# Barriers between the stages of a transformer block on eight cores, replaced by waits on single semaphores

## The chip, the cores and the metric

The kernel runs on all 8 cores of one Trainium2 chip. Each core computes two of the 16 sequences and shares nothing with the others. The metric is the device time of the slowest core, in microseconds (us), as the median over runs.

## The reference

One layer in the macaron form, on x of 16 x 2048 x 1024:

```python
x = x + 0.5 * ffn(layernorm(x))
x = x + attn(layernorm(x))
x = x + 0.5 * ffn(layernorm(x))
```

`ffn` is itself an attention, with 16 heads of width 64. A router (softmax of the mean of x @ Wr) picks 4 heads per sequence and a gate for each; Q, K and V of these four, times the gate, go through full softmax attention, and the 256 columns through Wo. `attn` is differential attention:

```python
q = apply_rotary(rmsnorm(x @ Wq.T), cos, sin) / sqrt(64)   # 16 half heads
k = apply_rotary(rmsnorm(x @ Wk.T), cos, sin)
attn = softmax(causal(q @ k))                              # 2048 x 2048
attn = attn[:, :, 0] - lam * attn[:, :, 1]                 # 8 heads
out = layernorm(attn @ v) * (1 - LAMBDA_INIT)
return out @ Wproj.T
```

## The kernel before, in words

`emit_all` (L1083) writes the program of each engine as a list; `wait` (L173) puts a wait for a semaphore's value into an engine's list. Each engine goes through its list in order. There is a semaphore for each of TensorE (`self.PE`), ScalarE (`self.ACT`), VectorE (`self.DVE`) and GpSimd (`self.GPS`), counted up by their instructions. A DMA is issued from a queue: SyncE (`sp`, 8 channels in turn), GpSimd (`gps`, 4) or ScalarE (`act`, 4), and each channel is a semaphore. `wait_q` (L205) makes an engine wait for all DMAs so far of one queue. `barrier` makes every engine wait for all 20 semaphores at the values that they have at this place in the program, 20 waits in each list (fewer where a semaphore is still at 0).

```python
    def barrier_into(self, eng):
        for s in self.ALLSEM:
            self.wait(eng, s, s.n)
```

`ALLSEM` lists TensorE, ScalarE, VectorE, GpSimd, the channels of SyncE, those of GpSimd and those of ScalarE, in this order. DMAs that change the type (weights from float32 in HBM to bfloat16) are issued from GpSimd, DMA transposes from SyncE or ScalarE. `dma` issues at L195, `dmat`, the transpose, at L202; so every DMA has one of these two lines.

For each of the two sequences (batches) of a core:

1. x is loaded into `x_res` and stays there; a layer norm writes bfloat16 tiles to `lnx_d`, and eight transposes (`_ln_transposes`) bring them back as `reg_a`.
2. First FFN, written out in `emit_all`: router, the folding of the chosen heads' weights into `wselg` (`emit_wfold`), projections (`emit_ffn_qkv`: L523 for Q and K, L549 for V), attention in two pairs of heads and eight blocks of queries (`emit_ffn_attn`: scores L580, exponentials on ScalarE L592, times V L612), and the output (`emit_ffn_out`: store of `zstrip`, two transposes, L670), with the next layer norm's sums beside it and the transposes behind it. attn_wqT and attn_wkT are loaded there into `big_b`.
3. `emit_attn`: the transposes a second time, Q and K projections for 16 tiles of tokens (L759) with norm and rotation on VectorE and GpSimd, then attn_wvT into `big_b` and the V projection (L782). `emit_attn_core` goes through eight heads: transposes of Q and K into `qk_strm`, scores (L926) against the blocks allowed by the mask, exponentials (L946), times V (L967), fix-ups on VectorE, sixteen strips of normalisation per head (L1022), and a store to `zhat_d`. `emit_attn_out`: eight transposes of `zhat_d` into `big_b` from SyncE, attn_wpT into `wselg` and ffn_wqT into `qk_strm` from GpSimd, and the output projection (L1052), again with the sums of the next norm beside it.
4. `emit_ffn` for the second FFN, as the first, but with the transposes a second time, too; then y is stored.

Between these parts stand barriers. `emit_all` has them ahead of each part of the first FFN and behind it; `emit_attn` and `emit_ffn` have one at their start, ahead of each part and at the end. Two stand in a row where `emit_all`'s or `emit_attn`'s last meets the first of the next.

Of the kernel before, what the change touches and what calls it, by code (L numbers as in the profile page):

```python
# [76 lines left out]
class MK:  # L77
# [286 lines left out]
    def _ln_transposes(self):  # L364
        P = self
        P.wait_q("act", "act")
        P.wait_q("act", "sp")
        for c in range(NC):
            P.dmat("act", self.reg_a[:, c * S:(c + 1) * S], self.lnx_d[:, c * 128:(c + 1) * 128])
# [143 lines left out]
    def emit_ffn_qkv(self, b, ci):  # L513
        P = self
        evac_ms = [0, 0]
        for wi, dst, bslot in ((0, self.qsel, 0), (1, self.ksel, 2)):
# [128 lines left out]
    def emit_ffn_out(self, b, ci, fuse_ln=None):  # L645
        P = self
# [4 lines left out]
        zt = self.qk_strm[:, 0:2 * S]  # L651
        for c in range(2):
            P.dmat("sp", zt[:, c * S:(c + 1) * S], self.zffn_d[:, c * 128:(c + 1) * 128])
        P.dma("gps", self.qk_strm[:, 4096:6144].rearrange("p (c f) -> p c f", f=D), self.w["ffn_wo"].rearrange("(c p) f -> p c f", p=128))
        P.dma("gps", self.rowsb[0:1, 0:1024], self.w["ffn_bo"][None, :])
        wo = self.qk_strm[:, 4096:6144]
        if getattr(self, "_prefetch_attn_w", False):
            P.dma("gps", self.big_b[:, 0:NC * D].rearrange("p (c f) -> p c f", f=D),
                  self.w["attn_wqT"].rearrange("(c p) f -> p c f", p=128))
            P.dma("gps", self.big_b[:, NC * D:2 * NC * D].rearrange("p (c f) -> p c f", f=D),  # L660
                  self.w["attn_wkT"].rearrange("(c p) f -> p c f", p=128))
        P.wait_q("pe", "sp")
        P.wait_q("pe", "gps")
        res_ms = [0, 0]
# [26 lines left out]
    def emit_ffn(self, b, ci, skip_ln=False, next_ln=None, wq_prefetched=False):  # L691
        P = self
        self.barrier()
# [29 lines left out]
        self.barrier()  # L723
        self.emit_ffn_qkv(b, ci)
        self.barrier()
        self.emit_ffn_attn(b, ci)
        self.barrier()
# [3 lines left out]
    def emit_attn_qkv(self, b, w_prefetched=False):  # L731
        P = self
# [7 lines left out]
        P.wait_q("pe", "gps")  # L740
        wbq = self.big_b[:, 0:NC * D]
# [290 lines left out]
    def emit_attn_out(self, b, fuse_ln=None):  # L1032
        P = self
# [6 lines left out]
        if getattr(self, "_prefetch_ffn_w", False):  # L1040
            P.dma("gps", self.qk_strm[:, 0:8192].rearrange("p (c f) -> p c f", f=D),
                  self.w["ffn_wqT"].rearrange("(c p) f -> p c f", p=128))
# [26 lines left out]
    def emit_attn(self, b, skip_ln=False, next_ln=None, w_prefetched=False):  # L1069
        self.barrier()  # L1070
        if skip_ln:
            self._ln_transposes()
        else:
            self.emit_ln(b, with_router=False, tag=f"attn_{b}")
        self.barrier()
        self.emit_attn_qkv(b, w_prefetched=w_prefetched)
        self.barrier()
        self.emit_attn_core(b)
        self.barrier()
# [134 lines left out]
```

How the kernel before makes its waits and increments, by code:

```python
    def wait(self, eng, sem, val):  # L173
        if val > 0:
            self.q[eng].append(lambda e, s=sem, v=val: e.wait_ge(s.h, v))
# [15 lines left out]
    def dma(self, queue, out, in_, **kw):  # L191
        ch = self._chan(queue)
        v0 = ch.n
        self.on(queue, lambda e, o=out, i=in_, s=ch, w=v0, kw=kw: (
            e.wait_ge(s.h, w), e.dma_start(out=o, in_=i, **kw).then_inc(s.h, 16)))
        return ch, ch.inc(16)
# [1 line left out]
    def dmat(self, queue, out, in_):  # L198
        ch = self._chan(queue)
        v0 = ch.n
        self.on(queue, lambda e, o=out, i=in_, s=ch, w=v0: (
            e.wait_ge(s.h, w), e.dma_start_transpose(o, i).then_inc(s.h, 16)))
        return ch, ch.inc(16)
# [8 lines left out]
        def step(e, f=fn, s=sem, w=w):  # L212
            e.wait_ge(s.h, w)
            f(e).then_inc(s.h, 1)
# [12 lines left out]
    def pe(self, fn, inc=True):  # L227
        if inc:
            self.on("pe", lambda e, f=fn, s=self.PE: f(e).then_inc(s.h, 1))
            return self.PE.inc(1)
        self.on("pe", fn)
        return self.PE.n
```

## Time and profile before

| | us |
|---|---|
| median of the 2 timed runs | 4664.37 (4661.91 and 4666.83) |
| the profiled execution, its own time | 4639.7 |
| its span, core 6, the slowest | 4638.1 |
| spans of the eight cores | 4594.9 to 4638.1 |
| busy in the span: TensorE | 2575.3 |
| VectorE | 1446.3 |
| ScalarE | 1467.0 |
| GpSimd | 332.1 |

The profile is of one execution on its slowest core. "Busy" leaves out waits and DMA issues. The chain of waits is followed back from the last instruction, at each step to what released it; a piece "ACTq" or "SPq" is a queue's own instruction, L175 a wait, L202 a transpose's issue, "issue" is time in which nothing that the profile shows was waited for. PEclk, or granted clock, is TensorE's as a share of 2.4 GHz; DMA share is the busy share of the core's 16 DMA engines. Times count from the start of the span.

### The profile page before, as it was taken

The page shows a single profiled execution, that of the slowest core. Times are in us where ns is not written, and L with a number is a line of the kernel's source. Part 1 is how long each engine was busy: PE and PEld are TensorE (multiplying, and loading weights), DVE is VectorE, ACT ScalarE, POOL GpSimd, SP SyncE. Part 2 cuts the span into 40 slices and gives each one's busy share as a digit, 9 for nine tenths or more (in the row PEclk, how much of TensorE's full clock was granted, in tenths as well). Part 3 has the DMA queues.
Part 4 walks back from the last instruction along what each step waited for, and adds up shares of the span by engine and source line. Part 5 has one row for each costly group of instructions (what it writes and reads, how often), then busy time and mean ns, then how long its engine had stood idle before and what let it go on. Part 6 is the DMA issues. An engine that isn't in the chain of part 4 may idle for free.

```text
span 4638.1 us, 58267 instructions; the slowest of 8 cores (4594.9 to 4638.1 us)
## 1 busy us (share of the span) xinstructions
PE 2575.3 (56%) x18326; PEld 1257.5 (27%) x18326; DVE 1446.3 (31%) x3373; ACT 1467.0 (32%) x1602; POOL 332.1 (7%) x258
## 2 busy tenths in 40 slices
PE   2367426556565645277523775264565666443875
PEld 0134202124343311244101341021233434102441
DVE  3121135623333333121231212366234333331212
ACT  1007313305555510027110173133055545100370
POOL 0000005610000000000000000066000000000000
PEclk9575558777767777575565755587777767776655
DMA  4310340031101042500243103400301020424003
GB/s 115 71 19 2 60 109 30 37 87 21 37 19 37 6 77 60 85 1 1 89 124 64 19 1 60 109 35 36 86 19 37 19 37 6 77 70 76 1 1 96
DMA packets 421276, 224.72 MB, mean 48 GB/s; under 512 B 358230, under 2 KB 366678, under 8 KB 420978
## 3 DMA queue, kind: packets, MB, share of 16 engines
q1 hardware_dynamic: 214610, 109.55, 9.3%
q10 hardware_dynamic: 180224, 67.13, 6.4%
q0 software_dynamic: 26144, 44.31, 6.2%
q8 instruction: 158, 2.59, 0.2%
q14 instruction: 140, 1.15, 0.1%
HBM read 114.20 MB, written 79.76 MB: 42 GB/s over the span
## 4 chain that ended last, share of the span: by engine, by line
PE 36%; DVE 19%; ACT 15%; DMA 10%; issue 9%; ACTq 6%; SPq 3%; DVEq 1%; POOL 0%; POOLq 0%
ACT big_b L946 6%; ACT big_b L592 6%; PE pw L967 5%; ACTq L202 5%; PE pw L612 3%; PE pw L926 3%; SPq L202 3%; PE pw L670 3%; PE pw L523 3%; PE pw L1052 2%; PE pw L782 2%; PE pw L478 2%; PE pw L580 2%; PE pw L352 2%; PE pw L350 2%
## 5 line engine op out<-in xcount | busy, mean ns | idle before, releaser
L946 ACT ACTIVATE big_b<-pw,c 128x1024 bf16<-128x1024 f32 x576 | 641.2, 1113 | 667.3 <-PE pw L926 224.7
L592 ACT ACTIVATE big_b<-pw 128x1024 bf16<-128x1024 f32 x512 | 523.8, 1023 | 745.2 <-PE pw L580 719.2
L967 PE MATMUL pw<-vstrips,big_b 128*128 128x129 bf16 x4352 | 433.4, 256 | 432.8 <-ACT big_b L946 180.9
L967 PEld LDWEIGHTS pw<-vstrips,big_b 128*128 128x128 bf16 x4352 | 329.5, 115 | 564.9 <-issue 564.7
L759 PE MATMUL pw<-big_b,reg_a 128*128 128x512 bf16 x1024 | 280.8, 442 | 308.5 <-DMA reg_a<-lnx_d 167.2
L612 PE MATMUL pw<-vstrips,big_b 128*128 128x65 bf16 x4096 | 307.7, 241 | 156.0 <-ACT big_b L592 96.6
L926 PE MATMUL pw<-qk_strm 64*128 64x256 bf16 x2304 | 320.7, 330 | 33.8 <-DMA vstrips<-vhat_d 33.7
L612 PEld LDWEIGHTS pw<-vstrips,big_b 128*128 128x128 bf16 x4096 | 237.9, 126 | 359.5 <-issue 359.5
L580 PE MATMUL pw<-qk_strm 64*128 64x256 bf16 x2048 | 298.3, 404 | 10.6 <-issue 10.6
L317 ACT ACTIVATE scr<-x_res 128x1024 f32<-128x1024 f32 x96 | 101.4, 1057 | 545.1 <-DVE stats L315 418.8
L350 PE MATMUL pw<-scr,c 128*1 128x512 f32 x128 | 88.2, 779 | 281.6 <-DVE qk_bf L348 217.4
L759 PEld LDWEIGHTS pw<-big_b,reg_a 128*128 128x128 bf16 x1024 | 110.2, 110 | 479.1 <-issue 398.7
L635 DVE RECIPROCAL stats<-pw 128x2 f32<-128x2 f32 x128 | 21.9, 171 | 619.3 <-PE pw L612 612.6
L994 DVE RECIPROCAL stats<-pw 128x2 f32<-128x2 f32 x128 | 21.8, 171 | 609.1 <-PE pw L967 542.0
L670 PE MATMUL pw<-qk_strm 128*128 128x512 bf16 x256 | 132.1, 620 | 134.2 <-issue 116.7
L1052 PE MATMUL pw<-wselg,big_b 128*128 128x512 bf16 x512 | 115.0, 389 | 133.2 <-issue 66.9
L782 PE MATMUL pw<-big_b,reg_a 128*128 128x512 bf16 x512 | 114.9, 389 | 116.9 <-DMA big_b<-attn_wvT 116.9
L382 ACT COPY scr<-pw 1x512 f32<-1x512 f32 x4 | 2.3, 574 | 502.2 <-DMA reg_a<-lnx_d 502.2
L683 DVE SCALAR_TENSOR_TENSOR x_res<-pw,x_res 128x512 f32<-128x512 f32 x128 | 88.5, 692 | 195.9 <-PE pw L675 188.5
L315 DVE TENSOR_REDUCE stats<-x_res 128x1 f32<-128x1024 f32 x96 | 117.1, 1220 | 98.7 <-DMA x_res<-x 89.0
L478 PE MATMUL pw<-wselg,big_b 128*128 128x256 bf16 x640 | 96.6, 326 | 72.1 <-DMA big_b<-ffn_wkT 35.2
L926 PEld LDWEIGHTS pw<-qk_strm 64*128 64x128 bf16 x2304 | 101.7, 104 | 127.7 <-issue 81.1
(172 smaller groups left out, 2761.8 us busy)
## 6 DMA issues: line engine op xcount, KB each, us to landing
x_res<-x SPq DMA_DIRECT2D x2, 8192.0 KB
y<-x_res SPq DMA_DIRECT2D x2, 8192.0 KB
lnx_d<-qk_bf ACTq DMA_DIRECT2D x48, 256.0 KB, 2.0
lnx_d<-pt ACTq DMA_DIRECT2D x48, 256.0 KB, 2.1
vstrips<-vhat_d SPq DMA_DIRECT2D x16, 516.0 KB
big_b<-ffn_wkT POOLq DMA_DIRECT2D x4, 2048.0 KB, 17.4
big_b<-ffn_wvT POOLq DMA_DIRECT2D x4, 2048.0 KB, 23.1
zhat_d<-zstrip SPq DMA_DIRECT2D x16, 512.0 KB
```

The lines of the kernel that those rows point to most:

```text
L202: e.wait_ge(s.h, w), e.dma_start_transpose(o, i).then_inc(s.h, 16)))
L478: P.pe(lambda e, fs=fs, mc=mc, bank=bank: e.matmul(bank[:, 0:256], wb[:, mc * D + fs * 128: mc * D + (fs + 1) * 128], self.gsel[:, mc * 25 ...
L580: P.pe(lambda e, hp=hp, qh=qh, kt=kt, ki=ki, hi=hi, pw=pw: e.matmul(pw[:, hi * 512 + ki * 256:hi * 512 + (ki + 1) * 256], self.ksel[hi * 6 ...
L592: P.act(lambda e, pw=pw, g=g: e.activation(out=self.big_b[:, (g % 4) * 1024:(g % 4) * 1024 + 1024], in_=pw[:, 0:1024], func=AF.Exp, scale= ...
L612: first=first, last=last: e.matmul(ob[:, qi * 65:(qi + 1) * 65], self.big_b[:, (g % 4) * 1024 + hi * 512 + ki * 256 + qi * 128: (g % 4) * ...
L670: P.pe(lambda e, tt=tt, half=half, c=c, bank=bank: e.matmul(bank[:, 0:512], zt[:, c * S + tt * 128:c * S + (tt + 1) * 128], wo[:, c * 1024 ...
L759: P.pe(lambda e, tt=tt, fc=fc, half=half, bank=bank, wb=wb: e.matmul(bank[:, 0:512], self.reg_a[:, fc * S + tt * 128:fc * S + (tt + 1) * 128],
L782: P.pe(lambda e, tt=tt, fc=fc, half=half, bank=bank, wb=wb: e.matmul(bank[:, 0:512], self.reg_a[:, fc * S + tt * 128:fc * S + (tt + 1) * 128],
L926: qT=qT, kT=kT, is_last=is_last: e.matmul(pw[:, hi * 512 + ki * 256:hi * 512 + (ki + 1) * 256], kT[hi * 64:(hi + 1) * 64, kt * 128:(kt + 1 ...
L946: P.act(lambda e, pw=pw, g=g: e.activation(out=self.big_b[:, (g % 4) * 1024:(g % 4) * 1024 + 1024], in_=pw[:, 0:1024], func=AF.Exp, scale= ...
L967: vst=vst, first=first, last=last: e.matmul(ob[:, qi * 129:(qi + 1) * 129], self.big_b[:, (g % 4) * 1024 + hi * 512 + ki * 256 + qi * 128: ...
L1052: P.pe(lambda e, tt=tt, fc=fc, half=half, bank=bank: e.matmul(bank[:, 0:512], self.big_b[:, fc * S + tt * 128:fc * S + (tt + 1) * 128], wp ...
```

## The change

Eight barriers per batch go: the first of `emit_attn` and of `emit_ffn` (kept where the layer norm isn't skipped, which doesn't occur here), and in both those ahead of each part behind it. Waits of single engines take their place, in the callers and inside `_ln_transposes`, `emit_ffn_qkv`, `emit_ffn_out`, `emit_attn_qkv` and `emit_attn_out`. The barriers of `emit_all`, around the first FFN, and those at the end of `emit_attn` and `emit_ffn` stay. The diff in full:

```diff
@@ -365,6 +365,7 @@
         P = self
         P.wait_q("act", "act")
         P.wait_q("act", "sp")
+        P.wait("act", self.PE, self.PE.n)
         for c in range(NC):
             P.dmat("act", self.reg_a[:, c * S:(c + 1) * S], self.lnx_d[:, c * 128:(c + 1) * 128])
 
@@ -513,6 +514,7 @@
     def emit_ffn_qkv(self, b, ci):
         P = self
         evac_ms = [0, 0]
+        P.wait("pe", self.DVE, self.DVE.n)
         for wi, dst, bslot in ((0, self.qsel, 0), (1, self.ksel, 2)):
             base = wi * NC * 256
             for h in range(2):
@@ -649,18 +651,22 @@
               self.zstrip.rearrange("p (t c) -> p t c", c=256))
         P.wait_q("sp", "sp")
         zt = self.qk_strm[:, 0:2 * S]
+        P.wait("sp", self.PE, self.PE.n)
         for c in range(2):
             P.dmat("sp", zt[:, c * S:(c + 1) * S], self.zffn_d[:, c * 128:(c + 1) * 128])
+        P.wait("gps", self.PE, self.PE.n)
         P.dma("gps", self.qk_strm[:, 4096:6144].rearrange("p (c f) -> p c f", f=D), self.w["ffn_wo"].rearrange("(c p) f -> p c f", p=128))
         P.dma("gps", self.rowsb[0:1, 0:1024], self.w["ffn_bo"][None, :])
         wo = self.qk_strm[:, 4096:6144]
         if getattr(self, "_prefetch_attn_w", False):
+            P.wait("gps", self.PE, self.PE.n)
             P.dma("gps", self.big_b[:, 0:NC * D].rearrange("p (c f) -> p c f", f=D),
                   self.w["attn_wqT"].rearrange("(c p) f -> p c f", p=128))
             P.dma("gps", self.big_b[:, NC * D:2 * NC * D].rearrange("p (c f) -> p c f", f=D),
                   self.w["attn_wkT"].rearrange("(c p) f -> p c f", p=128))
         P.wait_q("pe", "sp")
         P.wait_q("pe", "gps")
+        P.wait("pe", self.DVE, self.DVE.n)
         res_ms = [0, 0]
         for tt in range(NT):
             P.wait("pe", self.DVE, res_ms[tt % 2])
@@ -690,7 +696,8 @@
 
     def emit_ffn(self, b, ci, skip_ln=False, next_ln=None, wq_prefetched=False):
         P = self
-        self.barrier()
+        if not skip_ln:
+            self.barrier()
         if skip_ln:
             self._ln_transposes()
         else:
@@ -720,11 +727,13 @@
             P.wait_q("pe", "gps")
             self.emit_wfold(2, "ffn_bv", 4, slot=0)
         self.tap(f"wsel_{b}_{ci}", self.wsel[:, :])
-        self.barrier()
+        P.wait("pe", self.DVE, self.DVE.n)
+        P.wait_q("pe", "act")
         self.emit_ffn_qkv(b, ci)
-        self.barrier()
+        P.wait("pe", self.DVE, self.DVE.n)
+        P.wait("act", self.DVE, self.DVE.n)
         self.emit_ffn_attn(b, ci)
-        self.barrier()
+        P.wait("pe", self.DVE, self.DVE.n)
         self.emit_ffn_out(b, ci, fuse_ln=next_ln)
         self.barrier()
 
@@ -738,6 +747,7 @@
             P.dma("gps", self.big_b[:, NC * D:2 * NC * D].rearrange("p (c f) -> p c f", f=D),
                   self.w["attn_wkT"].rearrange("(c p) f -> p c f", p=128))
         P.wait_q("pe", "gps")
+        P.wait("pe", self.DVE, self.DVE.n)
         wbq = self.big_b[:, 0:NC * D]
         wbk = self.big_b[:, NC * D:2 * NC * D]
         ev_q = [0, 0]
@@ -1038,6 +1048,7 @@
                    self.zhat_d.rearrange("(h t p) d -> h (t p) d", h=NH, p=128)[c])
         P.dma("gps", self.wselg[:, 0:8192].rearrange("p (c f) -> p c f", f=D), self.w["attn_wpT"].rearrange("(c p) f -> p c f", p=128))
         if getattr(self, "_prefetch_ffn_w", False):
+            P.wait("gps", self.PE, self.PE.n)
             P.dma("gps", self.qk_strm[:, 0:8192].rearrange("p (c f) -> p c f", f=D),
                   self.w["ffn_wqT"].rearrange("(c p) f -> p c f", p=128))
         P.wait_q("pe", "sp")
@@ -1067,16 +1078,21 @@
             self._ln_finish(with_router=(fuse_ln == "router"))
 
     def emit_attn(self, b, skip_ln=False, next_ln=None, w_prefetched=False):
-        self.barrier()
         if skip_ln:
             self._ln_transposes()
         else:
+            self.barrier()
             self.emit_ln(b, with_router=False, tag=f"attn_{b}")
-        self.barrier()
+        P = self
+        P.wait("pe", self.DVE, self.DVE.n)
+        P.wait_q("pe", "act")
         self.emit_attn_qkv(b, w_prefetched=w_prefetched)
-        self.barrier()
+        P.wait_q("sp", "sp")
+        P.wait("dve", self.GPS, self.GPS.n)
         self.emit_attn_core(b)
-        self.barrier()
+        P.wait_q("sp", "sp")
+        P.wait("sp", self.PE, self.PE.n)
+        P.wait("act", self.PE, self.PE.n)
         self.emit_attn_out(b, fuse_ln=next_ln)
         self.barrier()
```

No instruction changes its place on its engine; what changes is what it waits for. Where the waits stand out, the instruction lists show them in brackets, `s_` for an engine's semaphore and `d_` for a channel's.

SyncE, end of the attention core in the first batch (`zhat_d<-zstrip` are the stores of heads, `big_b<-zhat_d` the transposes for the output projection), with - and + for before and now:

```order
 L195 DMA zhat_d<-zstrip 128x16x128 [waits s_dve,d_sp2]
 L195 DMA zhat_d<-zstrip 128x16x128 [waits s_dve,d_sp3]
-L202 DMA_TRANSPOSE big_b<-zhat_d 128x2048 [waits s_pe,s_act,s_dve,s_gps,d_sp0,d_sp1,d_sp2,d_sp3,d_sp4,d_sp5,d_sp6,d_sp7,d_gp0,d_gp1,d_gp2,d_gp3,d_ac0,d_ac1,d_ac2,d_ac3]
+L202 DMA_TRANSPOSE big_b<-zhat_d 128x2048 [waits d_sp0,d_sp1,d_sp2,d_sp3,d_sp4,d_sp5,d_sp6,d_sp7,s_pe]
 L202 DMA_TRANSPOSE big_b<-zhat_d 128x2048 [waits d_sp5]
 L202 DMA_TRANSPOSE big_b<-zhat_d 128x2048 [waits d_sp6]
```

The first transpose still waits for the last store's channel, and for TensorE, but for no load of GpSimd or ScalarE.

GpSimd, from the last rotation of K to the loads of the second FFN, first batch, before:

```order
L865 TENSOR_TENSOR vstrips<-vstrips,sinb_bf 128x512 [waits s_gps]
L866 TENSOR_TENSOR vprod<-vstrips 128x16x32 [waits s_gps]
L195 DMA big_b<-attn_wvT 128x8x1024 [waits s_pe,d_gp1]
L195 DMA wselg<-attn_wpT 128x8x1024 [waits s_pe,s_act,s_dve,s_gps,d_sp0,d_sp1,d_sp2,d_sp3,d_sp4,d_sp5,d_sp6,d_sp7,d_gp0,d_gp1,d_gp2,d_gp3,d_ac0,d_ac1,d_ac2,d_ac3]
L195 DMA qk_strm<-ffn_wqT 128x8x1024 [waits d_gp3]
```

and now:

```order
L875 TENSOR_TENSOR vstrips<-vstrips,sinb_bf 128x512 [waits s_gps]
L876 TENSOR_TENSOR vprod<-vstrips 128x16x32 [waits s_gps]
L195 DMA big_b<-attn_wvT 128x8x1024 [waits s_pe,d_gp1]
L195 DMA wselg<-attn_wpT 128x8x1024 [waits d_gp2]
L195 DMA qk_strm<-ffn_wqT 128x8x1024 [waits s_pe,d_gp3]
```

attn_wpT has lost the waits that stood between it and attn_wvT, among them those for the core's end; ffn_wqT waits for TensorE's last matmul of the core.

TensorE, start of FFN attention in the second FFN, first batch (L549 and L554, now L551 and L556, are the last tile of V, L580, now L582, the first scores), before:

```order
L549 MATMUL pw<-wselg,reg_a 128x256 [waits s_dve]
L549 MATMUL pw<-wselg,reg_a 128x256 x7
L554 MATMUL pw<-rowsb,cbf 128x256
L580 MATMUL pw<-qk_strm 128x256 [waits s_pe,s_act,s_dve,s_gps,d_sp0,d_sp1,d_sp2,d_sp3,d_sp4,d_sp5,d_sp6,d_sp7,d_gp0,d_gp1,d_gp2,d_gp3,d_ac0,d_ac1,d_ac2,d_ac3]
L580 MATMUL pw<-qk_strm 128x256 x7
```

and now:

```order
L551 MATMUL pw<-wselg,reg_a 128x256 [waits s_dve]
L551 MATMUL pw<-wselg,reg_a 128x256 x7
L556 MATMUL pw<-rowsb,cbf 128x256
L582 MATMUL pw<-qk_strm 128x256 [waits s_dve]
L582 MATMUL pw<-qk_strm 128x256 x7
```

Of twenty waits one is left, for VectorE.

## Rows read from the trace of the kernel before

**Rows 1.** The page, part 4: shares of the chain of waits by engine

```profile
PE 36%; DVE 19%; ACT 15%; DMA 10%; issue 9%; ACTq 6%; SPq 3%; DVEq 1%; POOL 0%; POOLq 0%
```

**Rows 2.** Chain of waits, end of the first attention core: start us, us, what

```profile
1644.37 4.86 DMA zhat_d<-zstrip
...
1650.35 2.12 SPq L202
...
1652.57 14.03 SPq L202
...
1666.69 14.01 SPq L202
...
1692.99 4.68 DMA big_b<-zhat_d
...
1698.65 57.61 PE pw L1052 x256
```

**Rows 3.** Timeline of GpSimd: start us, us, engine, line, operation, idle before

```profile
1650.56 0.87 POOL L195 DMA_DIRECT2D wselg<-attn_wpT  x1 [699.60 <-issue]
```

**Rows 4.** DMA issues in 1640 to 1702 us: size, us from issue to landing

```profile
wselg<-attn_wpT POOLq DMA_DIRECT2D x1, 2048.0 KB, 16.9
qk_strm<-ffn_wqT POOLq DMA_DIRECT2D x1, 2048.0 KB, 29.2
```

**Rows 5.** Busy time by stretch (engines, granted clock, DMA share, GB/s)

```profile
core 6: us, PE busy (x) PEld busy (x) DVE busy (x) ACT busy (x) POOL busy (x), PEclk, DMA share, GB/s
...
1650.35:1697.67 47.32, 0.00 (x0) 0.00 (x0) 0.00 (x0) 0.00 (x0) 1.75 (x2) 0.50 1.07 177
1840.86:1864.17 23.31, 0.00 (x0) 0.00 (x0) 0.00 (x0) 0.00 (x0) 0.00 (x0) 0.55 0.95 180
1866.34:1913.71 47.37, 0.00 (x0) 0.00 (x0) 0.00 (x0) 0.00 (x0) 1.38 (x2) 0.50 1.03 170
```

**Rows 6.** Timeline of TensorE and VectorE at the end of the core

```profile
1631.88 0.51 PE L967 MATMUL pw<-vstrips,big_b 128*128 128x129 bf16 x6 [1.01 <-ACT big_b L946]
...
1637.56 6.67 DVE L1022 TENSOR_SCALAR zstrip<-zstrip,stats 128x128 bf16<-128x128 bf16 x16 [1.03 <-ACT stats L1017]
```

**Rows 7.** Chain of waits, the same place in the second batch

```profile
3958.28 3.82 DMA zhat_d<-zstrip
3963.32 3.24 SPq L202
...
4007.65 4.35 DMA big_b<-zhat_d
```

**Rows 8.** Chain of waits, load of attn_wvT ahead of the V projection

```profile
950.02 14.17 DMA big_b<-attn_wvT
964.64 57.68 PE pw L782 x256
```

**Rows 9.** Chain of waits, ScalarE queue, two barriers in a row, first and last

```profile
1864.19 0.02 ACTq L175
...
1866.29 0.02 ACTq L202
```

**Rows 10.** Chain of waits, TensorE behind the barriers of the second FFN

```profile
1978.17 0.14 issue
...
1979.19 2.33 issue
...
2040.27 2.10 issue
```

**Rows 11.** Chain of waits on SyncE behind FFN attention, first and last

```profile
2224.88 0.02 issue
...
2225.84 0.02 SPq L195
```

**Rows 12.** Busy time by stretch around the start of FFN attention

```profile
2042.00:2046.00 4.00, 2.35 (x32) 1.40 (x32) 0.00 (x0) 2.85 (x3) 0.00 (x0) 0.80 0.00 0
2042.40:2225.00 182.60, 142.16 (x1536) 79.04 (x1536) 23.63 (x96) 130.96 (x128) 0.00 (x0) 0.51 0.01 1
```

## The prediction

> **What bounds the kernel now.** I began with the spans of the cores (4594.9 to 4638.1 us, so all eight behave alike), then the page's chain of waits, then that chain in order of time. No engine bounds the whole: TensorE has 36% of the chain, VectorE 19%, ScalarE 15% [rows 1]; the work goes through stages with a barrier between them. So I looked for stretches in which no engine works. In the chain in order of time the longest is at the end of the attention core. The last matmul of the core ends at 1632.39 us and VectorE's last strip at 1644.23 [rows 6]. Then come the store of the last head (4.86 us), eight DMA transposes issued from 1650.35, of which two each hold the queue 14 us, and the first matmul of the output projection at 1698.65 [rows 2]. GpSimd had been idle for 700 us and issued attn_wpT and ffn_wqT at 1650.56 and right behind it [rows 3]; they landed 16.9 and 29.2 us later [rows 4]. The DMA engines are full in that stretch (share 1.07). Eight transposes of the same size with nothing beside them took 23.3 us, and eight beside two such weight loads 47.4 us [rows 5]. The second batch has the same picture [rows 7].
>
> **The change, part by part.** All durations are from one profiled execution of 4639.7 us (span 4638.1), 24.7 us under the median of the runs shown, 4664.4; a saving worked out in the first is taken off the second.
>
> *The end of the core.* The barrier ahead of emit_attn_out goes. On GpSimd's queue attn_wpT now stands directly behind attn_wvT, with no wait but its own channel's: it is issued near 951 us instead of 1650, and a load alone lands in 14.2 us [rows 8], so it lies beside the V projection (57.7 us [rows 8]), which needs the queues little. ffn_wqT overwrites qk_strm, which the core reads, so it waits for TensorE alone and not for VectorE and the store: issued near 1632.6 instead of 1651.4. Alone it would land between 1632.6 + 14.2 = 1646.8 (the row of attn_wvT) and 1632.6 + 16.9 = 1649.5 (attn_wpT's, which had company). Both are before 1650.35. So the eight transposes lose both companions: 47.32 us become 23.3, a gain of 24.0. Against it, ffn_wqT now shares the DMA engines with the last store for 2.4 to 5.1 us; the store can be late by none of it or all; I take 2 us. The wait list of the first transpose becomes shorter (21 waits after the store in 1.1 us before, 14 after): 0.4 us. The first batch gains 24.0 - 2 + 0.4 = 22.4 us. In the second the stretch was 3963.32 to 4012.00, 48.7 us [rows 7], so 48.7 - 23.3 - 2 + 0.4 = 23.8. Together 46.2 us. Bounds: 50.6 with no delay of the store and 0.4 more per batch, and below, if only one of the two loads leaves the stretch, half of 24.0 + 25.4, which is 24.7.
>
> *Loads moved, and what they pass.* What attn_wpT could hurt is attn_wvT just ahead of it, for which TensorE waits. Two loads issued together landed 12.3 us apart [rows 4], so they go one after the other; I take 0. The bounds are 0 and 12.0 us per batch. Ahead of ffn_wo only TensorE is waited for now, some 4 us earlier; it lies beside a store and two transposes: 0.
>
> *The waits themselves.* A barrier is up to 20 waits on each engine. Where all were long satisfied they still cost issue time: on ScalarE 34 waits of two barriers and what follows took 2.1 us [rows 9], some 0.055 us each; on SyncE, behind FFN attention, 18 in 0.96 us [rows 11]. The doubled barriers ahead of emit_attn's and emit_ffn's transposes stand on the chain on ScalarE: 20 waits less and one more each, 2 x 1.05 = 2.1 us per batch. TensorE is slower at it: it took 2.33 us from VectorE's last write to the first matmul of the FFN's projections and 2.10 us to that of FFN attention, where a single wait costs 0.14 us [rows 10]. 17 waits followed the one on VectorE, so about 0.12 each; six remain in the first place (0.8 us with the 0.14) and one in the second (0.2): 1.5 + 1.9 = 3.4 us. SyncE ahead of the FFN's store 0.9 us; ahead of the core 0.3. The barrier ahead of attn_qkv costs nothing, since ScalarE's channels, the last of its list, are what TensorE waits for there either way. Sum 6.7 us per batch, 13.4 for two. Bounds: 4 (TensorE's waits overlapping other latency) and 16.
>
> *Waits added.* TensorE on VectorE, ScalarE on TensorE and on VectorE, SyncE on TensorE, VectorE on GpSimd: each stands where the store, the transposes or the load ahead lands later than what it asks for, or where a barrier stays. Behind ScalarE's wait ahead of the transposes stand only these; it asks for matmuls that end before the last store has landed. I take 0 and bound it at 0.5 us each, the core's last group of matmuls [rows 6].
>
> Sum: 46.2 + 13.4 = 59.6 us, so 4639.7 becomes 4580.1, and 4664.4 becomes 4604.8.
>
> The Trainium skill, "SBUF — State Buffer", section "SBUF: two separate sides", says that a DMA issued from GpSimd has its descriptors written by GpSimd, and that VectorE in a two-port mode locks it out of the ports for it, so that the DMA sits and waits. VectorE runs sixteen bf16 strips from 1637.56 to 1644.23 in this stretch, 5 us after the new issue of ffn_wqT [rows 6]. By that rule the load could stand still until 1644.2 and run beside the transposes; no run here has such a load beside such strips. By the sum without it the load has landed by then.
>
> **The rivals.**
> 1. Only attn_wpT leaves the stretch; ffn_wqT starts, but moves its bytes only once VectorE's strips are done at 1644.2, and still lies beside the transposes. For it: VectorE is busy through most of the new window [rows 6]. Against: they begin 5 us after the issue, and GpSimd's part of an issue took 0.87 us [rows 3]. Gain at the core 24.7: 24.7 + 13.4 = 38.1, time 4626. The rule quoted above would give this. The same price, within 3 us, if attn_wvT is slowed by the load behind it (59.6 - 24.0 = 35.6, time 4629). Together 0.18.
> 2. The change doesn't do what it says: the transposes of zhat_d are slow by themselves, and not for the loads. Against: the two of 14 us stand exactly beside the loads, and once the second of them is through, at 1680.7, all that is left lands within 17 us [rows 2]. Then only 13.4 + 0.8 are gained, time 4650. Chance 0.05.
> 3. Slower than before, through TensorE's clock: the output projection took 57.6 us for 256 matmuls [rows 2], 225 ns each, after a start at the low level. If it ran whole at half the granted clock, with 450 ns each, it would take 57.6 us more per batch, 115 in all: 4604.8 + 115 = 4720, slower than before. It decides once more than half of the two projections (59.6 of 115 us) runs so. Against: TensorE idles there before and after the change, and the shorter idle time gives no reason to stay low. Chance 0.02.
> 4. Faster, through the clock at the start of FFN attention: the granted clock was 1.00, 0.80 on average in the first 4 us, and 0.51 over the stage's 182.6 us [rows 12]. Just ahead TensorE stood idle, 2.1 us of it behind the barrier [rows 10], of which the change leaves 0.2. If the clock stays at 2.4 GHz, the stage is bound by ScalarE's 131 us [rows 12] and by the 16 drains between blocks of queries, say 1 us each, so 147: 35 us in each of the two second FFNs, 70 in all, time 4535. But the slowest of eight cores would have to keep it for both stages, and each drain can end it. Chance 0.04. A part of it on some cores doesn't show in the slowest.
>
> **How the numbers follow.** My forecast has 0.71. The low end takes 50.6 + 16 = 67 us off, 7 more than the forecast, and then 30 for what one execution differs from another (4639.7 to 4666.8 in the three shown) and for a core that keeps the clock for part of FFN attention: 4568. The high end is the first rival with some 14 us for the spread: 4640. It leaves out rivals 2 to 4, 0.11. About 2%, 93 us, is what a measurement of this kernel tells from no change. Only rival 4 passes it below: 0.04. Nothing named passes 4758 above; 0.01 for what I don't see. The rest, 0.95, lies within.
>
> **What would show it.** In the changed kernel: attn_wpT issued right behind attn_wvT near 950 us and landed before 980; ffn_wqT issued within 1 us of the core's last matmul; the eight transposes of zhat_d in 23 to 25 us, none with 14; the first matmul of the output projection some 43 us after the core's last instead of 66; TensorE's gap ahead of FFN attention, in the second FFN alone, near 1 us. Wrong: a load that lands after the first transposes have begun, a store of zhat_d over 8 us, an attn_wvT of over 20 us, or FFN attention in the second FFN at another clock than in the first.

## The result and the profile after

| | before | changed |
|---|---|---|
| median, us | 4643.3 (10 runs) | 4562.18 (11 runs, 4556.66 to 4604.97) |
| ratio, 95% interval | 1 | 0.9843 [0.9808, 0.9877] |
| the changed kernel run again with the experiments, us | 4646.96 (11 runs) | 4559.92 (6 runs, ratio 0.9832 [0.9782, 0.9883]) |
| busy in the span: TensorE, VectorE, ScalarE, GpSimd | 2575.3, 1446.3, 1467.0, 332.1 | 2559.8, 1447.3, 1468.1, 331.9 |

0.9843 of 4643.3 is a saving of 73 us, 57 to 89 by its interval; forecast were 59.6. It lies within 2%, as forecast; the second series gives 78 us, with an interval that reaches a little beyond 2%. In some executions of either kernel the cores of one die show a lower granted clock and the time is longer, which the ratios leave out, and as the first profiled execution of the changed kernel was one of them, the rows below are from the second series (4558.45 us; core 0, the slowest).

The page, its header, part 1 and part 4:

```profile
span 4556.8 us, 56773 instructions; the slowest of 8 cores (4532.1 to 4556.8 us)
...
PE 2559.8 (56%) x18326; PEld 1244.0 (27%) x18326; DVE 1447.3 (32%) x3373; ACT 1468.1 (32%) x1602; POOL 331.9 (7%) x258
...
PE 37%; DVE 19%; ACT 16%; DMA 10%; issue 9%; ACTq 6%; SPq 2%; DVEq 1%; POOL 0%; POOLq 0%
```

Busy times are as they were but for 16 us of TensorE. The transposes' issues ("SPq") have gone from 3% of the chain to 2% [rows 1]: the work is the same, and a piece of the waiting is gone.

The chain of waits at the end of the attention core (start us, us, what), first batch, and in the second:

```profile
1642.23 4.98 DMA zhat_d<-zstrip
...
1647.98 2.05 SPq L202
...
1650.12 2.71 SPq L202
...
1663.48 2.14 SPq L202
...
1665.71 4.09 DMA big_b<-zhat_d
...
1670.81 56.99 PE pw L1063 x256
...
3905.28 7.11 DMA zhat_d<-zstrip
...
3915.16 3.48 SPq L202
...
3932.75 4.24 DMA big_b<-zhat_d
```

These answer to [rows 2] and [rows 7]. Where two transposes held the queue 14 us each, all eight of the first batch now hold it 2.0 to 2.7 us, and from the first issue to the last landing pass 1669.80 - 1647.98 = 21.8 us instead of 47.3. It is the same on the eight cores in both batches: before, the second and the third transpose held the queue 12.4 to 18.5 us each (once 25.2); now none holds it more than 3.9, and the eight take 20.2 to 25.4 us. The first matmul of the projection comes 1670.81 - 1630.27 = 40.5 us behind the core's last:

```profile
1629.76 0.51 PE L977 MATMUL pw<-vstrips,big_b 128*128 128x129 bf16 x6 [1.01 <-ACT big_b L956]
1670.81 9.49 PE L1063 MATMUL pw<-wselg,big_b 128*128 128x512 bf16 x36 [40.54 <-issue]
...
1635.45 6.64 DVE L1032 TENSOR_SCALAR zstrip<-zstrip,stats 128x128 bf16<-128x128 bf16 x16 [1.03 <-ACT stats L1027]
```

The columns are start, duration, engine, line, operation, and in brackets the idle time ahead of it, here 40.54 us. VectorE's sixteen strips and what stands before them are as in [rows 6].

DMA issues (size each, us from issue to landing) in 1625 to 1700 us and in 940 to 975 us:

```profile
qk_strm<-ffn_wqT POOLq DMA_DIRECT2D x1, 2048.0 KB, 14.5
...
big_b<-attn_wvT POOLq DMA_DIRECT2D x1, 2048.0 KB, 17.5
wselg<-attn_wpT POOLq DMA_DIRECT2D x1, 2048.0 KB, 27.5
```

And GpSimd's timeline:

```profile
940.60 0.94 POOL L195 DMA_DIRECT2D big_b<-attn_wvT  x1
941.53 0.88 POOL L195 DMA_DIRECT2D wselg<-attn_wpT  x1
...
1630.87 0.88 POOL L195 DMA_DIRECT2D qk_strm<-ffn_wqT  x1 [688.46 <-PE pw L977]
```

attn_wpT stands right behind attn_wvT; ffn_wqT is released by "PE pw L977", the core's last matmul [rows 3, 4]. Both loads are out of the transposes' way, as the prediction has it.

The second FFN. The chain at the start of its projections (first two rows) and of its attention (the other two):

```profile
1947.02 0.17 DVE rowbuf L511
1947.19 0.77 issue
...
2005.53 0.44 DVE vstrips L559
2005.96 0.14 issue
```

From VectorE's last write to the first matmul 0.77 and 0.14 us, instead of 2.33 and 2.10 [rows 10]. And the clock in that attention (busy time by stretch: us, then TensorE, its weight loads, VectorE, ScalarE and GpSimd, each with its count, granted clock, DMA share, GB/s):

```profile
2006.00:2061.00 55.00, 42.97 (x471) 23.87 (x472) 5.91 (x24) 40.29 (x40) 0.00 (x0) 0.52 0.01 1
```

It is at the 1.2 GHz level, as in [rows 12], though the wait ahead of it is gone.

One collision of the same kind is left. At the start of `emit_ffn` the second set of transposes of `lnx_d` runs beside the loads of ffn_wkT and ffn_wvT, as it did before [rows 5, last line]. GpSimd's timeline, then the chain of waits:

```profile
1836.57 0.88 POOL L195 DMA_DIRECT2D big_b<-ffn_wkT  x1 [204.82 <-DMA reg_a<-lnx_d]
...
1836.82 1.27 ACTq L202
1838.17 30.62 ACTq L202
```

The loads wait for the first set of transposes, at the barrier that stays at the end of `emit_attn`, and so start together with the second set.

To see where all of it went I added up, on each of the eight cores, the time between the last matmul of a stage and the first of the next. Medians of the eight, us, first batch / second batch:

| between | before | changed |
|---|---|---|
| core and output projection | 66.8 / 66.2 | 41.1 / 42.0 |
| folding and projections, second FFN | 2.7 / 2.7 | 1.1 / 1.2 |
| projections and attention, second FFN | 2.7 / 2.7 | 0.8 / 0.8 |
| attention and output, second FFN | 20.2 / 19.4 | 18.8 / 18.3 |
| FFN output and Q/K projections of `emit_attn` | 84.3 / 84.1 | 82.9 / 82.6 |
| last norm sum and folding, second FFN | 94.4 / 94.5 | 93.8 / 95.2 |
| Q/K and V projections | 59.6 / 58.7 | 60.8 / 59.7 |
| V projection and core | 16.7 / 16.0 | 16.9 / 15.4 |
| the same two gaps of the first FFN (projections; attention), untouched, first batch | 2.6 and 2.6 | 2.6 and 2.6 |

Without the last row the table is a saving of 60.4 us, 49.9 of it at the end of the core. (In the second batch the first FFN's gap ahead of its projections went from 2.6 to 2.9.) Against the 73 of the ratio, some 13 us have no place in it. They lie within the ratio's interval, and the runs of before that the ratio uses lie up to 61 us apart (4617.0 to 4678.3 in one series).

Part of them is how far the slowest core stands from the others. Between the two profiled executions the slowest span fell by 81.3 us, the median of the eight by 70.1 (4620.1 to 4550.0): the slowest stood 18.0 us above the median before and 6.8 after. Of the 70.1, 60.4 are in the table and about 10 are spread over the rest, 5 of them inside the stages. It is alike in the runs that the second ratio compares: their means differ by 77.9 us, and with the median of the eight cores in place of the slowest by 70.7. "By the median core" means this second reckoning below. Why the slowest core is nearer to the others stays open.

### The profile page after: what moved, and what is told of

It reads as the page before. It is cut to its first block, busy times and chain, and to the rows that moved or that the text cites. A ratio compares the mean times of both kernels' runs of the same rounds, so it can differ in the third digit from the quotient of the medians.

```text
span 4641.7 us, 56709 instructions; the slowest of 8 cores (4560.2 to 4641.7 us)
## 1 busy us (share of the span) xinstructions
PE 2670.6 (58%) x18262; PEld 1286.2 (28%) x18326; DVE 1447.1 (31%) x3373; ACT 1468.2 (32%) x1602; POOL 331.7 (7%) x258
## 4 chain that ended last, share of the span: by engine, by line
PE 39%; DVE 18%; ACT 15%; DMA 10%; issue 9%; ACTq 6%; SPq 2%; DVEq 1%; POOL 0%; POOLq 0%
ACT big_b L956 6%; ACT big_b L594 6%; PE pw L977 6%; ACTq L202 5%; PE pw L936 4%; PE pw L614 3%; PE pw L792 3%; PE pw L1063 3%; PE pw L525 3%; PE pw L676 3%; PE pw L582 2%; PE pw L479 2%; PE pw L352 2%; PE pw L350 2%; DVE zstrip L1032 2%
## 5 line engine op out<-in xcount | busy, mean ns | idle before, releaser
L977 PE MATMUL pw<-vstrips,big_b 128*128 128x129 bf16 x4352 | 456.7, 265 | 417.3 <-ACT big_b L956 181.6
L977 PEld LDWEIGHTS pw<-vstrips,big_b 128*128 128x128 bf16 x4352 | 346.7, 119 | 558.7 <-issue 558.5
L769 PE MATMUL pw<-big_b,reg_a 128*128 128x512 bf16 x1002 | 278.7, 442 | 307.6 <-DMA reg_a<-lnx_d 164.9
L614 PE MATMUL pw<-vstrips,big_b 128*128 128x65 bf16 x4096 | 307.2, 240 | 155.9 <-ACT big_b L594 95.2
L936 PE MATMUL pw<-qk_strm 64*128 64x256 bf16 x2304 | 336.1, 345 | 32.8 <-DMA vstrips<-vhat_d 32.5
L614 PEld LDWEIGHTS pw<-vstrips,big_b 128*128 128x128 bf16 x4096 | 237.0, 125 | 359.5 <-issue 359.5
L582 PE MATMUL pw<-qk_strm 64*128 64x256 bf16 x2048 | 298.3, 404 | 6.7 <-issue 5.2
L1004 DVE RECIPROCAL stats<-pw 128x2 f32<-128x2 f32 x128 | 21.8, 171 | 633.9 <-PE pw L977 555.5
L637 DVE RECIPROCAL stats<-pw 128x2 f32<-128x2 f32 x128 | 21.8, 171 | 614.7 <-PE pw L614 607.9
L792 PE MATMUL pw<-big_b,reg_a 128*128 128x512 bf16 x502 | 137.1, 444 | 123.1 <-DMA big_b<-attn_wvT 122.2
L1063 PE MATMUL pw<-wselg,big_b 128*128 128x512 bf16 x500 | 135.9, 442 | 80.7 <-issue 79.8
```

The costliest lines, as they stand in the source:

```text
L582: P.pe(lambda e, hp=hp, qh=qh, kt=kt, ki=ki, hi=hi, pw=pw: e.matmul(pw[:, hi * 512 + ki * 256:hi * 512 + (ki + 1) * 256], self.ksel[hi * 6 ...
L614: first=first, last=last: e.matmul(ob[:, qi * 65:(qi + 1) * 65], self.big_b[:, (g % 4) * 1024 + hi * 512 + ki * 256 + qi * 128: (g % 4) * ...
L769: P.pe(lambda e, tt=tt, fc=fc, half=half, bank=bank, wb=wb: e.matmul(bank[:, 0:512], self.reg_a[:, fc * S + tt * 128:fc * S + (tt + 1) * 128],
L792: P.pe(lambda e, tt=tt, fc=fc, half=half, bank=bank, wb=wb: e.matmul(bank[:, 0:512], self.reg_a[:, fc * S + tt * 128:fc * S + (tt + 1) * 128],
L936: qT=qT, kT=kT, is_last=is_last: e.matmul(pw[:, hi * 512 + ki * 256:hi * 512 + (ki + 1) * 256], kT[hi * 64:(hi + 1) * 64, kt * 128:(kt + 1 ...
L977: vst=vst, first=first, last=last: e.matmul(ob[:, qi * 129:(qi + 1) * 129], self.big_b[:, (g % 4) * 1024 + hi * 512 + ki * 256 + qi * 128: ...
```

## The experiments

**The changed kernel again.** No edit.

> The changed kernel once more, beside the others. Theory (the loads leave the transposes' stretch: 46 us; queues' waits: 13 us): 60 us under before, ratio 0.987; in its profile the eight transposes of zhat_d take 23 us, ffn_wqT lands before the first of them is issued. Rival (the clock gives part of the gain at the start of FFN attention): 75 us or more under before, and the granted clock of the second FFN's attention is over 0.55 on most cores.

Measured: 0.9832 [0.9782, 0.9883], and the rows above. The 78 us are more than the 75 of the rival, but not by its way: the granted clock over the second FFN's attention is 0.51 on all eight cores.

**Only the end of the core.** In before, the barrier ahead of `emit_attn_out` alone is replaced, with the wait for ffn_wqT:

```diff
         self.emit_attn_core(b)
-        self.barrier()
+        P = self
+        P.wait_q("sp", "sp")
+        P.wait("sp", self.PE, self.PE.n)
+        P.wait("act", self.PE, self.PE.n)
```

> Only the barrier between attention core and output projection is replaced; all others stay. Theory: 46 us of the gain, ratio 0.990, first matmul of the output projection some 43 us behind the core's last. Rival (all removed barriers matter alike, some 8 us each in sum of the engines' restarts): 15 us, ratio 0.997. Rival (the gain needs attn_wpT to be issued as early as behind attn_wvT; here the barrier ahead of the core holds it until near 1027 us): no difference is expected from that by the theory, since it lands 600 us ahead of its use.

Measured: 0.9946 [0.9891, 1.0002], 25 us where 46 were expected, by the time alone not told from none; the gaps between the stages tell more. The stretch at the end of the core did shrink as in the changed kernel, to 41.6 and 41.2 us. But the one ahead of the core, from the V projection to its first matmul, grew from 16.7 to 28.9 and from 16.0 to 27.2 us. GpSimd's timeline and then the chain of waits there (core 2) show why:

```profile
1033.31 0.87 POOL L195 DMA_DIRECT2D wselg<-attn_wpT  x1 [80.99 <-issue]
```

```profile
1032.41 3.39 SPq L202
...
1035.90 12.86 SPq L202
...
1049.48 8.36 DMA qk_strm<-qhat_d
```

The barrier ahead of the core still stands in GpSimd's list between attn_wvT and attn_wpT, so attn_wpT goes out at 1033.31, together with the core's first transposes, and the second of those holds the queue 12.86 us. On all cores and in both batches it is 9.8 to 14.5 us, where the same transpose takes 1.8 to 3.5 in before and in the changed kernel. I had expected nothing from that barrier. In before it costs next to nothing; it costs 12 us per batch once the later one is gone.

**All but the end of the core.** The barrier ahead of `emit_attn_out` is put back into the changed kernel:

```diff
         self.emit_attn_core(b)
+        self.barrier()
         P.wait_q("sp", "sp")
```

> The changed kernel with the one barrier at the core's end put back, ahead of all that follows. Theory: only the queues' waits are saved, 13 us, ratio 0.997, and the stretch from the core's last matmul to the projection is 66 us as before, with two transposes of 14 us. Rival (the rest of the change is worth more than its waits, as the measured 73 us against the forecast 60 may hint): 25 us or more, ratio 0.9945 or less.

Measured: 0.9956 [0.9906, 1.0007], 20 us; the end of the core at 66.4 and 66.3 us, as before, the other gaps of the table 19 us less in sum. 14 of them are in the rows that the forecast names (projections, attention and output of the second FFN, Q/K projections of `emit_attn`), near its 13.4; the other 5 are in rows that move by 1 to 2 us from run to run with no edit there. The two halves add up to 25 + 20 = 45 us by their ratios, the whole is 73 to 78; the 2 x 12 us of the collision ahead of the core, which only the whole avoids, are most of what is missing, though each ratio is known to some 25 us only. By the median core the halves are 27 and 20 us and the whole 71, so 24 are missing.

**The end and the start of the core.** To show that it is this pair, before with these two barriers replaced and no other (and the wait for ffn_wqT, as above):

```diff
         self.emit_attn_qkv(b, w_prefetched=w_prefetched)
-        self.barrier()
+        P = self
+        P.wait_q("sp", "sp")
+        P.wait("dve", self.GPS, self.GPS.n)
         self.emit_attn_core(b)
-        self.barrier()
+        P.wait_q("sp", "sp")
+        P.wait("sp", self.PE, self.PE.n)
+        P.wait("act", self.PE, self.PE.n)
```

> The kernel before with the barriers at both ends of the attention core replaced, all others kept. The run with the core's end alone started the core 12 us later, since attn_wpT was issued with the first transposes of the core. Theory: attn_wpT goes behind attn_wvT again, the wait ahead of the core is 16 us, the one behind it 42, and the gain is 50 us, ratio 0.989. Rival (something else in that run delayed the core): the wait ahead of the core stays at 28 us, ratio 0.9945.

Measured: 0.9893 [0.9845, 0.994], 50 us. The gap ahead of the core is 16.5 and 15.4 us again, its end 42.7 and 40.5, and attn_wpT goes out at once behind attn_wvT, as GpSimd's timeline (core 1) shows:

```profile
952.56 0.94 POOL L195 DMA_DIRECT2D big_b<-attn_wvT  x1
953.50 0.89 POOL L195 DMA_DIRECT2D wselg<-attn_wpT  x1
```

**ffn_wqT late.** In the changed kernel ffn_wqT alone waits for what the barrier asked for, all 20 semaphores as they stand at the end of the core:

```diff
+        at_end = [(s, s.n) for s in self.ALLSEM]
...
         if getattr(self, "_prefetch_ffn_w", False):
-            P.wait("gps", self.PE, self.PE.n)
+            for s, v in at_end:
+                P.wait("gps", s, v)
```

> The changed kernel, but ffn_wqT is issued only when everything up to the core's end is done, the last store included; attn_wpT stays early. Theory (each load beside the transposes costs its own 12 us of full DMA engines): 12 us more per batch than the changed kernel, 24 in all, so 35 us under before, ratio 0.9925; the eight transposes take 35 us, one of them 14. Rival (the transposes suffer only when two loads stand beside them): like the changed kernel, 60 us under before. Rival (one load is as bad as two): 13 us under before.

Measured: 0.9878 [0.982, 0.9936], 57 us; the end of the core 51.1 and 51.8 us, 10 us more than in the changed kernel in each batch. The chain of waits there (core 5), then GpSimd's timeline:

```profile
1653.44 3.87 DMA zhat_d<-zstrip
...
1658.08 2.30 SPq L202
...
1660.48 11.34 SPq L202
```

```profile
1658.63 0.88 POOL L195 DMA_DIRECT2D qk_strm<-ffn_wqT  x1 [706.17 <-issue]
```

One load beside the eight transposes, issued 0.6 us behind the first of them, makes one of them 11.3 us long; two made two of 14 [rows 2]. On the eight cores in both batches it is the second transpose each time, 11.0 to 12.5 us, with 4.0 to 4.4 for the one behind it. So a load beside the transposes costs some 10 us per batch, where 12 were expected; the first rival would have cost that.

**More barriers.** The price of a barrier by itself: before, with three more barriers at each of the seven other places in `emit_attn` and `emit_ffn`.

```diff
+    def more(self):
+        for _ in range(3):
+            self.barrier()
...
         self.barrier()
+        self.more()
         self.emit_ffn_attn(b, ci)
```

> The kernel before, with three more barriers right behind each of its seven that the change drops elsewhere than at the core's end. Theory (a barrier whose semaphores are all reached costs its waits' issue: 1.1 us in a row on ScalarE or SyncE, 2.0 to 2.4 on TensorE): per batch three times 1.1 + 1.1 on ScalarE's places, 2.3 + 2.3 + 2.3 on TensorE's, 1.0 + 1.0 on SyncE's, 33 us, 66 in all, ratio 1.014. Rival (they overlap other latency and are nearly free): under 15 us, ratio under 1.003. Rival (a barrier is a real drain and costs more than its waits): over 120 us.

Measured: 1.0115 [1.0061, 1.0169], 53 us. The gaps at the seven places are 54.6 us longer in sum, where 66 were expected. Per batch: 6.5 ahead of the FFN's projections, 6.4 ahead of its attention, 8.6 and 7.9 ahead of `emit_attn`'s Q/K projections (two places in a row), 2.1 and 2.8 ahead of the core, 2.5 and 1.6 at the start of `emit_ffn`, 1.6 ahead of the FFN's output. In the chain of waits the two on TensorE are:

```profile
2013.35 0.17 DVE rowbuf L514
2013.52 8.82 issue
...
2080.60 0.44 DVE vstrips L561
2081.04 8.47 issue
```

8.82 - 2.33 and 8.47 - 2.10 are 6.5 and 6.4 us for 60 waits: 0.107 us for a wait that is satisfied, 2.1 us for a barrier, on TensorE. Where the chain goes through the lists of SyncE or ScalarE it is a quarter to a half of it: 1.6 / 3 = 0.5 us ahead of the FFN's output, 0.7 to 0.9 ahead of the core. The 8.6 and 7.9 us are of six barriers, three on ScalarE's list ahead of the transposes and three on TensorE's behind them (there 6.71 us pass on core 5 from the last transpose's landing to the first matmul, 0.59 in before).

**One set of transposes.** What the removed barriers left standing in a row: the eight transposes of `lnx_d` are issued twice, with the same result, at the end of the stage and at the start of the next. In the changed kernel the second set goes, in `emit_attn` and likewise in `emit_ffn`:

```diff
-        if skip_ln:
-            self._ln_transposes()
-        else:
+        if not skip_ln:
```

> The changed kernel without the second set of the eight transposes of lnx_d at the start of emit_attn and of emit_ffn (the first set, at the end of the layer norm, has brought the same data). Theory: 24 us less per batch ahead of the attention's projections, and ahead of the second FFN the router starts 47 us earlier, so that its weight loads, 29 us, become what the folding waits for: about 39 us less. Together 63 per batch, 125 in all, so 190 us under before, ratio 0.959. Rival (the loads of ffn_wkT and ffn_wvT stay what counts there): 24 + 10 per batch, ratio 0.972.

Measured: 0.9571 [0.952, 0.9622], near 121 us less than the changed kernel by the medians, 135 by the median core; 125 were expected. The gap ahead of the Q/K projections fell from 82.9 to 58.4 us (57.8 in the second batch), the one at the start of `emit_ffn` from 93.8 and 95.2 to 52.7 and 51.9. That is 24.6 us per batch at the first place and 41 to 43 at the second, 134 in all. At the second more goes than a set costs, since there the set stood beside two loads, as shown above. So a barrier and the second set together were the waste at these two places; the change took the 1 us and left the 24 and more.

**FFN attention with wide V matmuls.** The fourth rival says that this stage would be 35 us shorter at the high clock. In the changed kernel, in all four FFNs, its matmuls with V compute 128 columns instead of 65, of which 63 are not used, so that TensorE has more to do; the block of two outputs lies 256 apart.

```diff
+                                wide = min(128, 4160 - (h * 1040 + kt * 65))
...
-                                    ob[:, qi * 65:(qi + 1) * 65],
+                                    ob[:, qi * 256:qi * 256 + wide],
...
-                                    self.vstrips[:, h * 1040 + kt * 65: h * 1040 + (kt + 1) * 65],
+                                    self.vstrips[:, h * 1040 + kt * 65: h * 1040 + kt * 65 + wide],
```

> The changed kernel with the matmuls with V in both FFN attentions 128 columns wide instead of 65 (the columns beyond are written beside the results and not used), to ask whether TensorE's clock has something to give there. Theory (the clock falls at the stage's start and stays low whatever the matmuls' width): each of the four stages 181 us becomes some 215, the whole 130 us slower than the changed kernel, ratio 1.013. Rival (with wider matmuls TensorE keeps the granted clock at 1.00 for most of the stage): the stage is bound by ScalarE, some 150 us, the whole 120 us faster than the changed kernel, ratio 0.958.

Measured: 0.9775 [0.9724, 0.9826]; neither. Busy time by stretch (core 3), in the first FFN and in the second:

```profile
345.00:400.00 55.00, 38.02 (x496) 24.30 (x496) 8.41 (x35) 42.00 (x42) 0.00 (x0) 1.00 0.01 1
...
2060.00:2110.00 50.00, 34.94 (x460) 22.23 (x454) 7.38 (x30) 39.30 (x39) 0.00 (x0) 1.00 0.01 1
```

The granted clock stays at 2.4 GHz in these stretches; over the four whole stages it is 0.96 to 0.99 on every core, where it was 0.50 to 0.52. TensorE's busy share is 0.69 in the first stretch (0.71 over the whole stages), less than the 0.78 at 1.2 GHz in the rows of the changed kernel; the matmuls compute nearly twice the columns and it is done sooner. But the stage only fell from 181.4 to 170.0 us, not to 147. ScalarE's timeline of one block of queries, up to the first exponentials of the next:

```profile
367.46 2.14 ACT L594 ACTIVATE big_b<-pw 128x1024 bf16<-128x1024 f32 x2 [1.29 <-PE pw L582]
369.89 2.14 ACT L594 ACTIVATE big_b<-pw 128x1024 bf16<-128x1024 f32 x2 [0.28 <-PE pw L582]
372.20 2.14 ACT L594 ACTIVATE big_b<-pw 128x1024 bf16<-128x1024 f32 x2 [0.18 <-ACT big_b L594]
374.52 2.14 ACT L594 ACTIVATE big_b<-pw 128x1024 bf16<-128x1024 f32 x2 [0.17 <-ACT big_b L594]
377.95 2.14 ACT L594 ACTIVATE big_b<-pw 128x1024 bf16<-128x1024 f32 x2 [1.29 <-PE pw L582]
```

A block takes 377.95 - 367.46 = 10.49 us, 16 of them 168: that is the stage. 8.2 us of it are eight exponentials; 1.29 us ScalarE waits for TensorE at the turn of the block, which is the drain (1 was taken), and 1.0 us lies between the exponentials within it, which the estimate of 147 had left out. So a stage at the high clock is shorter, as the fourth rival has it, but with these wider matmuls by 11 us and not by 35: 43 in the four stages. What it would gain with matmuls of 65 columns at the high clock no run shows, nor whether the width holds the clock or the new place of the outputs. By the ratios the run is worth 26 us against the changed kernel, 31 by the medians, with intervals of some 24 us on each, and 42 by the median core.

**Both, and the first FFN too.** The wide V matmuls with one set of transposes, then also the three barriers inside the first FFN, in `emit_all`, replaced by the waits that the second has:

```diff
...
             if phases >= 5:
-                self.barrier()
+                self.wait("pe", self.DVE, self.DVE.n)
+                self.wait("act", self.DVE, self.DVE.n)
                 self.emit_ffn_attn(b, 0)
...
```

> The changed kernel with one set of transposes only and with matmuls with V 128 columns wide: what the runs so far point to. Theory (stages stand one behind the other, so the gains add): ratio 0.957 from the one set, and 11 us less in each of four FFN attentions, 44 in all, so ratio 0.948, 240 us under before. Rival (the wide matmuls' gain was partly chance, as its ratio to the changed kernel, 0.994, is only 28 us): ratio 0.951.

> The same, and the three barriers of the first FFN are replaced as in the second. Theory (its waits alone are saved): 1.5 + 2.0 + 1.3 = 4.8 us per batch, 10 in all, below what a measurement tells, but seen in the profile: 1.1 us instead of 2.6 ahead of the first FFN's projections and 0.75 instead of 2.6 ahead of its attention, on all cores. Rival (the load of attn_wqT and attn_wkT, issued earlier now, delays the store of zffn_d): the wait behind the first FFN's attention, 45 us, becomes longer and eats the 10 us.

Measured: 0.9441 [0.9404, 0.9478], 4378.2 us, and 0.9431 [0.9394, 0.9469], 4373.85 us. The first is the sum of its parts within the intervals (0.9571 less what the wide matmuls gave, 26 to 43 us, is 0.951 to 0.948, and the parts' own intervals are 0.005 to either side). The second step is 4 us by the medians, not told apart from none; in its trace the gaps of the first FFN are 1.1 and 0.75 us instead of 2.6 and 2.6, which makes some 7 us for two batches. The gap behind the first FFN's attention, which the rival has longer, is 43.8 and 41.7 us instead of 42.7 and 42.1: it didn't come. This version beats both kernels. Its page, header and part 4:

```profile
span 4374.7 us, 56088 instructions; the slowest of 8 cores (4343.5 to 4374.7 us)
...
PE 35%; DVE 19%; ACT 19%; DMA 12%; issue 8%; ACTq 3%; SPq 1%; DVEq 1%; POOL 0%; POOLq 0%
```

ScalarE has now 19% of the chain, and its queue 3% instead of 6.

## Why the prediction was right, and where its steps were off

**The loads leave the transposes: right, and its size too.** From the last store's landing to the last transpose's, medians of eight cores: 48.7 us before in both batches, 23.8 and 24.7 after. That is 24.9 and 24.0 us, against 24.0 + 0.4 and 25.4 + 0.4. With ffn_wqT alone late, 10 us of it are lost again, with the barrier alone put back all of it: shown from both sides. The second rival (transposes slow by themselves) has fallen.

**The store's delay: wrong, by some 4 us in all.** I had taken 2 us per batch for the last store, which shares the DMA engines with ffn_wqT. Its median went from 5.0 to 4.1 us in the first batch and from 3.8 to 4.8 in the second, with one of 7.1: nothing in sum. This is why the end of the core gave 49.9 us and not 46.2; the bound of 50.6 held (by its own terms, 46.2 + 4 + 0.8, it is 51.0).

**ffn_wqT beside VectorE's strips: the first rival didn't come.** It was issued at 1630.87, 0.6 us behind the core's last matmul; VectorE's strips ran from 1635.45 to 1642.09, and it landed 14.5 us after its issue, at 1645.4, ahead of the first transpose at 1647.98. On the eight cores in both batches it took 13.3 to 16.8 us, and landed ahead of the transposes each time. attn_wvT, with no such strips beside it, took 14.2 in [rows 8], which is the shortest of the eight cores (up to 17.4 us). The Trainium skill, "SBUF — State Buffer", section "SBUF: two separate sides", would have such a load wait for its descriptors while VectorE is in a two-port mode. This case doesn't show it: sixteen strips of 128x128 bf16, begun 5 us behind the issue, delayed nothing that these times could tell. It doesn't refute the rule either, since GpSimd's part, 0.87 us, was over by then.

**attn_wpT behind attn_wvT: taken as 0, measured as 1.** attn_wvT landed 17.5 us after its issue on this core; the median of the eight went from 15.6 to 16.9 us in the first batch and from 15.2 to 15.7 in the second, and the gap ahead of the V projection grew from 59.6 to 60.8 and from 58.7 to 59.7. The prediction's reading behind the 0, two loads landed 12.3 us apart, is of times from issue to landing; the landings themselves lay 1680.6 - 1667.5 = 13.1 us apart [rows 3, 4].

**The barriers' waits: right in sum, not in every place.** Forecast 13.4. TensorE ahead of the projections 1.5 of 1.5, ahead of FFN attention 2.0 of 1.9, the doubled barrier ahead of `emit_attn` 1.4 of 1.05; SyncE ahead of the FFN's output 1.3 of 0.9. The one at the start of `emit_ffn` gave nothing that can be read (+0.6 and -0.7 of 1.05), with a spread of 4 us over the cores there. 0.12 us for a wait on TensorE was 0.107 by itself.

**The split that was wrong: "ahead of the core 0.3".** I had priced each barrier by the time that its waits take in before. For this one that is right, and it is wrong for the change: what makes attn_wpT early is not that the barrier at the core's end goes, but that both go. The prediction's sum holds since the change removes both; what it said of the order on GpSimd's queue ("directly behind attn_wvT") had this in it. But whoever had split the 46 us by the steps would have given them all to one barrier, as I did for the run above, and been off by 12 us per batch.

**The clock.** The third rival (slower, with the projection at the low level) hasn't come: 57.0 us for its 256 matmuls. The fourth hasn't either: the 2 us of idle time ahead of FFN attention are gone, the clock falls all the same. Its price was too high as well, as far as the wide matmuls tell: 11 us per stage where 35 were written.

**The total.** 4604.8 was forecast for a before of 4664.4, and 4562.18 measured beside a before of 4643.3. Of the 42.6 us between, 21.1 are the other level of before. The other 21.5 are the medians' difference of 81.1 less the 59.6 forecast; 8 of them are gone if the ratio of 0.9843 is taken, 1 is the table of gaps, and the rest is what stands behind the table: the slowest core, nearer to the others, and small pieces of no one place. As a time 4562.18 lies 6 us under the low end of 4568; carried over to the before of the forecast, 4664.4 x 0.9843 = 4591, it lies inside. No term of the prediction has the slowest core coming nearer to the others; the 30 us that its range left for the spread took that in, and not its sum.

## What to carry to other kernels

A barrier costs its waits, here 0.1 us each on TensorE and less elsewhere, only where its engine is on the chain; what it may cost besides is the start of every DMA that stands behind it in a queue that nothing else holds. So look for the queue whose next issue could be early, and follow it back past every barrier between, not only the last one: removing only the last one here moved the collision to the next stage and gave back half of what it had won. And when barriers stand twice in a row, look at what work stands twice between them.

## What the runs showed of the hardware

- Eight DMA transposes of 128 x 2048 took 21 to 26 us from the last store's landing to theirs with no load beside them, 10 more with one load of 2 MB, 24 more with two (medians of eight cores), and most of it was in one transpose's issue per load, while the queue stood: 12.4 to 18.5 us twice with two loads (once 25.2), 11.0 to 12.5 once with one, 9.8 to 14.5 for a transpose at the core's start, where it is 1.8 to 3.5 otherwise.
- A wait for a semaphore that has long reached its value took 0.107 us on TensorE (60 waits, 6.4 to 6.5 us).
- FFN attention ran at the 1.2 GHz level with V matmuls of 65 columns, TensorE busy for 0.78 of the time, and at 2.4 GHz with 128 columns, busy for 0.71. Computing columns that nobody reads made the stage 11 us shorter. Which property of the work the clock follows these runs don't show.
